# A fused attention and FP4 layer on one core: another order of the same steps on all five queues

## What is computed

```
xn = layernorm(x)
s  = attention block(xn): per head, scores = causal_kern[i-j] + qm[i] + km[j] + 0.15/sqrt(8) * qc[i].kc[j]
     (causal), softmax, times v; out projection; ln1(xn + .); ffn 256 -> 1024 -> 256 with gelu; ln2
     causal_kern comes from the mean of xn over each batch, a top-8 choice of 16 kernels, and a window
f  = fp4_linear(silu(fp4_linear(xn, w_gate)) * fp4_linear(xn, w_up), w_down)      256 -> 704 -> 256
     fp4_linear rounds both operands to FP4 (E2M1) in blocks of 16, with a scale per block
out = x + s * silu(f)
```

## Time and profile before

| | us |
|---|---|
| median of 3 runs | 1921.82 (1917.81 to 1922.19) |
| profiled execution, first to last instruction | 1916.1 |
| median above that span | 5.7 |
| first `out` matmul (L733) of all | 234.2 |
| one period of the mid part | 109.8 |
| from the last period to the end | 144.0 |

### The profile page before, as it was taken

How to read it: one execution, slowest core, us unless ns; L and a number is a source line. 1 busy time by engine, 2 the same in 40 slices (tenths; PEclk the granted TensorE clock), 3 DMA queues, 4 the chain that set the end, 5 groups by cost and what they waited for, 6 DMA issues and landing times.

```text
span 1916.1 us, 37547 instructions
## 1 busy us (share of the span) xinstructions
PE 1822.3 (95%) x12803; PEld 1311.7 (68%) x12803; DVE 1590.4 (83%) x5143; ACT 930.2 (49%) x1939; POOL 1095.4 (57%) x797
## 2 busy tenths in 40 slices
PE   7888999999999999999999999999999999999987
PEld 3335677777767767676776767677776767677766
DVE  6788899788888989888888978888897988888863
ACT  3635454544546354544635454453645445463542
POOL 2446657465556647464665746565664756466562
PEclk8999999999999999999999999999999999999999
DMA  5534233232322233232223323233222333322211
GB/s 156 165 96 114 64 91 83 75 110 75 99 75 79 76 82 115 75 90 73 91 74 93 93 75 110 64 102 79 83 77 75 110 84 91 75 85 74 61 57 34
DMA packets 138646, 166.69 MB, mean 87 GB/s; under 512 B 19757, under 2 KB 100654, under 8 KB 138452
## 3 DMA queue, kind: packets, MB, share of 16 engines
q1 hardware_dynamic: 138458, 164.30, 30.5%
HBM read 127.85 MB, written 36.41 MB: 86 GB/s over the span
## 4 chain that ended last, share of the span: by engine, by line
PE 50%; DVE 26%; issue 12%; POOL 4%; DMA 3%; ACT 3%; SPq 2%; DVEq 0%; POOLq 0%; ACTq 0%
PE ps L760 8%; PE ps L769 7%; PE ps L701 7%; PE ps L718 4%; DVE Pr L1067 3%; PE ps L624 3%; PE ps L597 3%; PE ps L733 3%; PE ps L658 3%; PE ps L674 2%; DVE nmax L1037 2%; POOL slot L1215 2%; PE ps L654 2%; DMA Tz<-kernel_rows 2%; DVE st L958 2%
## 5 line engine op out<-in xcount | busy, mean ns | idle before, releaser
L1176 POOL TENSOR_TENSOR Pr<-Pr,Tz 128x768 f32<-128x768 f32 (+2 forms) x384 | 477.6, 1273 | 233.8 <-ACT Pr L833 230.0
L1037 DVE CUSTOM_DVE_ANT_0 ps<-ps,future 128x512 f32<-128x512 f32 (+3 forms) x1024 | 474.5, 516 | 52.9 <-issue 51.8
L833 ACT ACTIVATE Pr<-ps 128x384 f32<-128x384 f32 x512 | 243.1, 489 | 345.2 <-PE ps L658 343.9
L760 PE MATMUL ps<-catT,w 128*128 128x256 f32 x1024 | 237.8, 380 | 0.7 <-ACT catT L896 0.7
L769 PE MATMUL ps<-w,gT 128*128 128x256 f32 x1024 | 232.9, 381 | 0.9 <-ACT gT L913 0.9
L624 PE MATMUL ps<-KS,QS 108*128 108x512 bf16 (+3 forms) x1024 | 215.0, 300 | 17.9 <-DVE nmax L1037 13.2
L822 ACT ACTIVATE ps<-ps 128x512 f32<-128x512 f32 x256 | 150.5, 588 | 137.7 <-PE ps L654 136.1
L1067 DVE SCALAR_TENSOR_TENSOR Pr<-ps,Tz 128x512 f32<-128x512 f32 x256 | 175.3, 685 | 46.2 <-ACT ps L822 41.0
L769 PEld LDWEIGHTS ps<-w,gT 128*128 128x128 f32 x1024 | 190.8, 190 | 25.7 <-ACT gT L913 1.3
L760 PEld LDWEIGHTS ps<-catT,w 128*128 128x128 f32 x1024 | 189.6, 190 | 26.2 <-ACT catT L896 0.9
L718 PE MATMUL ps<-wdT,hqT 128*128 128x256 f32 x768 | 179.5, 383 | 0.7 <-ACT hqT L872 0.7
(11 more groups left out here) (239 smaller groups left out, 3270.0 us busy)
## 6 DMA issues: line engine op xcount, KB each, us to landing
Tz<-kernel_rows SPq DMA_DIRECT2D x256, 256.0 KB, 3.6
KS<-k_parts SPq DMA_DIRECT2D x32, 384.0 KB
QS<-q_parts SPq DMA_DIRECT2D x64, 192.0 KB
hY<-in_x SPq DMA_DIRECT2D x19, 512.0 KB, 5.1
xn<-in_x SPq DMA_DIRECT2D x17, 512.0 KB, 3.8
out<-y SPq DMA_DIRECT2D x15, 512.0 KB, 2.9
q_parts<-q_sp SPq DMA_DIRECT2D x16, 384.0 KB, 3.0
k_parts<-k_sp SPq DMA_DIRECT2D x16, 384.0 KB, 2.4
```

The source lines that it names most:

```text
L760: ins = mm(dst[:, i * n:(i + 1) * n], w1[:, c, f * P:(f + 1) * P], catT[:, c, hf * n:(hf + 1) * n], start=c == 0, stop=c == KD - 1)
L833: inc(af(Pr[:, p % 4, e, at:at + wd], src[:, 0:wd], ACT.Exp), "a_exp")
L1037: ins = v.tensor_tensor_reduce(o, o, future[:, S - n:S], -1.0, 3e38, ALU.add, ALU.min, nmax[:, 2 * pl + e, it:it + 1])
L1176: ins = g.tensor_tensor(a, a, Tz[:, p % 2, :, P * j:P * j + PAST[j]], ALU.mult)
```

## The change

All five orders are written anew, in head, mid and end, with the same steps: none is added or removed, and no instruction within a step changes. `psum_plan` now counts the uses of each ring through the whole unrolled program, so a bank goes with the pair (batch, use) and no longer with (part, use); with 49 uses of the first ring, its two banks change places from one period to the next. `bank_for` and the `bank` functions look the bank up by batch.

The mid part whole:

```diff
     mid=dict(
         sync="""
-            T.0 load.1 T.1 T.2 xload T.3 mio.1 T.4 splitio T.5 load.0 T.6 T.7 fin mio.0
+            T.1 T.0 load.1 T.2 xload T.3 T.4 mio.1 T.5 splitio load.0 T.6 T.7 fin mio.0
         """,
         gpsimd="""
-            ln1 mul.0 lnb1 xnb mul.1 hq.0 mul.2 hr.0 projm.0 mul.3 hq.1 projm.1 hr.1 projm.2 xq xr mul.4 hq.2 mul.5
-            ln2 hr.2 fin mul.6 hq.3 mul.7 hr.3
+            ln1 lnb1 mul.0 xnb mul.1 hq.0 mul.2 hr.0 hq.1 mul.3 projm.0 projm.1 hr.1 projm.2 xq xr mul.4 hq.2 mul.5 hr.2
+            ln2 fin mul.6 hq.3 mul.7 hr.3
         """,
         vector="""
-            out.0 out.1 ln1 muld.0.0 silu.0.0 lnc1 silu.0.1 muld.0.1 mx.1.0.0 lnb1 mx.1.0.1 mx.1.0.2 muld.1.0 mx.1.0.3
+            out.0 out.1 ln1 muld.0.0 lnc1 silu.0.0 lnb1 muld.0.1 silu.0.1 mx.1.0.0 mx.1.0.1 muld.1.0 mx.1.0.2 mx.1.0.3
             silu.1.0 mx.1.0.4 mx.1.1.0 muld.1.1 mx.1.1.1 mx.1.1.2 mx.1.1.3 mx.1.1.4 muld.2.0 mx.1.2.0 mx.1.2.1 hq.0
-            mx.1.2.2 mx.1.2.3 norm mx.1.2.4 mx.1.3.0 muld.2.1 mx.1.3.1 mx.1.3.2 mx.1.3.3 mx.1.3.4 muld.3.0 mfin.1 hr.0
-            silu.1.1 f2.0 muld.3.1 proj.0 hq.1 f2.1 ctxt.0 proj.1 proj.2 muld.4.0 hr.1 xq muld.4.1 xr xr2 silu.2.0
-            muld.5.0 silu.2.1 hq.2 v.0 v.1 muld.5.1 f2.2 hr.2 mx.0.0.0 mx.0.0.1 f2.3 ln2 mx.0.0.2 mx.0.0.3 muld.6.0
-            silu.3.0 ctxt.1 muld.6.1 lnc2 lnb2 mx.0.0.4 mx.0.1.0 dn.0 silu.3.1 muld.7.0 mx.0.1.1 mx.0.1.2 mx.0.1.3
-            mx.0.1.4 hq.3 muld.7.1 mx.0.2.0 mx.0.2.1 mx.0.2.2 mx.0.2.3 mx.0.2.4 dn.1 ctxt.2 hr.3 mx.0.3.0 mx.0.3.1
-            dn.2 mx.0.3.2 mx.0.3.3 mx.0.3.4 mfin.0 ctxt.3 dn.3
+            mx.1.2.2 mx.1.2.3 norm mx.1.2.4 mx.1.3.0 muld.2.1 mx.1.3.1 mx.1.3.2 mx.1.3.3 mx.1.3.4 silu.1.1 muld.3.0
+            mfin.1 hr.0 muld.3.1 f2.0 hq.1 ctxt.0 proj.0 xq proj.1 proj.2 f2.1 hr.1 muld.4.0 silu.2.0 muld.4.1 xr xr2
+            silu.2.1 muld.5.0 v.0 hq.2 v.1 f2.2 muld.5.1 hr.2 f2.3 mx.0.0.0 mx.0.0.1 ln2 mx.0.0.2 muld.6.0 mx.0.0.3
+            silu.3.0 lnc2 mx.0.0.4 lnb2 muld.6.1 mx.0.1.0 dn.0 silu.3.1 mx.0.1.1 muld.7.0 mx.0.1.2 ctxt.1 mx.0.1.3
+            mx.0.1.4 hq.3 muld.7.1 mx.0.2.0 mx.0.2.1 mx.0.2.2 mx.0.2.3 mx.0.2.4 ctxt.2 dn.1 hr.3 mx.0.3.0 mx.0.3.1 dn.2
+            mx.0.3.2 mx.0.3.3 mx.0.3.4 mfin.0 ctxt.3 dn.3
         """,
         tensor="""
-            cT out.0 out.1 sc.0.0 gu.0.0 sc.0.1 gu.0.1 sc.0.2 sc.0.3 mx.1.0.0 mx.1.0.1 sc.0.4 gu.1.0 sc.0.5 mx.1.0.2
-            sc.1.0 hT sc.1.1 mx.1.0.3 sc.1.2 sc.1.3 mx.1.0.4 mx.1.1.0 sc.1.4 f1.0.0 mx.1.1.1 mx.1.1.2 f1.0.1 sc.1.5
-            sc.2.0 mx.1.1.3 mx.1.1.4 f1.0.2 mx.1.2.0 mx.1.2.1 f1.0.3 mx.1.2.2 mx.1.2.3 sc.2.1 sc.2.2 pv.0 sc.2.3
-            mx.1.2.4 mx.1.3.0 gu.1.1 mx.1.3.1 sc.2.4 xT.0 sc.2.5 sc.3.0 mx.1.3.2 xT.1 sc.3.1 ctxt.0 mx.1.3.3 mx.1.3.4
-            f2.0 mT.1 sc.3.2 sc.3.3 proj.0 sc.3.4 proj.1 proj.2 sc.3.5 f2.1 sc.4.0 sc.4.1 f1.1.0 tr.0.0 f1.1.1 f1.1.2
-            f1.1.3 sc.4.2 sc.4.3 gu.2.0 gu.2.1 sc.4.4 sc.4.5 v.0 sc.5.0 sc.5.1 v.1 f2.2 tr.0.1 sc.5.2 sc.5.3 f2.3
-            sc.5.4 sc.5.5 mx.0.0.0 mx.0.0.1 pv.1 sc.6.0 mx.0.0.2 mx.0.0.3 gu.3.0 sc.6.1 ctxt.1 sc.6.2 sc.6.3 mx.0.0.4
-            mx.0.1.0 sc.6.4 dn.0 sc.6.5 sc.7.0 gu.3.1 mx.0.1.1 pv.2 mx.0.1.2 sc.7.1 tr.1.0 mx.0.1.3 tr.1.1 mx.0.1.4
-            tr.2.0 sc.7.2 sc.7.3 mx.0.2.0 dn.1 sc.7.4 mx.0.2.1 sc.7.5 tr.2.1 mx.0.2.2 ctxt.2 mx.0.2.3 mx.0.2.4 dn.2
-            mx.0.3.0 mx.0.3.1 pv.3 mx.0.3.2 mx.0.3.3 xqT mx.0.3.4 tr.3.0 tr.3.1 ctxt.3 mT.0 dn.3
+            cT out.0 out.1 sc.0.0 gu.0.0 sc.0.1 gu.0.1 sc.0.2 sc.0.3 sc.0.4 gu.1.0 mx.1.0.0 mx.1.0.1 sc.0.5 sc.1.0 hT
+            sc.1.1 mx.1.0.2 mx.1.0.3 sc.1.2 sc.1.3 mx.1.0.4 mx.1.1.0 sc.1.4 f1.0.0 mx.1.1.1 mx.1.1.2 f1.0.1 mx.1.1.3
+            sc.1.5 sc.2.0 mx.1.1.4 f1.0.2 sc.2.1 mx.1.2.0 mx.1.2.1 sc.2.2 f1.0.3 sc.2.3 mx.1.2.2 mx.1.2.3 pv.0 mx.1.2.4
+            mx.1.3.0 gu.1.1 mx.1.3.1 xT.0 ctxt.0 sc.2.4 sc.2.5 mx.1.3.2 xT.1 sc.3.0 sc.3.1 mx.1.3.3 mx.1.3.4 f2.0 sc.3.2
+            sc.3.3 mT.1 proj.0 sc.3.4 proj.1 sc.3.5 f2.1 sc.4.0 proj.2 f1.1.0 f1.1.1 f1.1.2 sc.4.1 f1.1.3 gu.2.0 sc.4.2
+            tr.0.0 sc.4.3 gu.2.1 sc.4.4 sc.4.5 v.0 sc.5.0 f2.2 tr.0.1 sc.5.1 sc.5.2 v.1 sc.5.3 sc.5.4 f2.3 sc.5.5
+            mx.0.0.0 sc.6.0 mx.0.0.1 pv.1 mx.0.0.2 mx.0.0.3 gu.3.0 mx.0.0.4 tr.1.0 sc.6.1 sc.6.2 dn.0 sc.6.3 mx.0.1.0
+            sc.6.4 gu.3.1 mx.0.1.1 sc.6.5 sc.7.0 ctxt.1 mx.0.1.2 pv.2 mx.0.1.3 tr.1.1 sc.7.1 mx.0.1.4 tr.2.0 sc.7.2
+            sc.7.3 mx.0.2.0 dn.1 sc.7.4 mx.0.2.1 sc.7.5 ctxt.2 tr.2.1 mx.0.2.2 mx.0.2.3 mx.0.2.4 dn.2 mx.0.3.0 mx.0.3.1
+            pv.3 mx.0.3.2 mx.0.3.3 xqT mx.0.3.4 tr.3.0 tr.3.1 ctxt.3 mT.0 dn.3
         """,
         scalar="""
-            cT sc.0.0 vcopy silu.0.0 sc.0.1 silu.0.1 sc.0.2 sc.0.3 sc.0.4 sc.0.5 sc.1.0 hT silu.1.0 sc.1.1 sc.1.2
-            sc.1.3 sc.1.4 sc.1.5 sc.2.0 f1.0.0 f1.0.1 f1.0.2 f1.0.3 sc.2.1 sc.2.2 sc.2.3 ctxe.0 sc.2.4 xT.0 sc.2.5
-            silu.1.1 xT.1 sc.3.0 sc.3.1 mT.1 sc.3.2 sc.3.3 proj.0 projm.0 sc.3.4 proj.1 sc.3.5 proj.2 sc.4.0 sc.4.1
-            projm.1 projm.2 tr.0.0 f1.1.0 f1.1.1 f1.1.2 f1.1.3 sc.4.2 sc.4.3 sc.4.4 sc.4.5 silu.2.0 gscopy sc.5.0
-            sc.5.1 silu.2.1 sc.5.2 sc.5.3 sc.5.4 sc.5.5 tr.0.1 sc.6.0 ctxe.1 silu.3.0 sc.6.1 sc.6.2 sc.6.3 sc.6.4
-            sc.6.5 sc.7.0 dn.0 silu.3.1 ctxe.2 sc.7.1 tr.1.0 tr.1.1 sc.7.2 sc.7.3 sc.7.4 sc.7.5 tr.2.0 dn.1 tr.2.1
-            dn.2 ctxe.3 xqT tr.3.0 tr.3.1 mT.0 dn.3
+            cT vcopy sc.0.0 sc.0.1 silu.0.0 sc.0.2 sc.0.3 sc.0.4 silu.0.1 silu.1.0 sc.0.5 sc.1.0 sc.1.1 hT sc.1.2 sc.1.3
+            sc.1.4 sc.1.5 sc.2.0 sc.2.1 f1.0.0 f1.0.1 f1.0.2 f1.0.3 sc.2.2 ctxe.0 sc.2.3 xT.0 sc.2.4 sc.2.5 xT.1 gscopy
+            silu.1.1 sc.3.0 sc.3.1 sc.3.2 sc.3.3 mT.1 sc.3.4 sc.3.5 proj.0 proj.1 proj.2 sc.4.0 projm.0 projm.1 f1.1.0
+            f1.1.1 projm.2 f1.1.2 f1.1.3 sc.4.1 silu.2.0 sc.4.2 sc.4.3 sc.4.4 silu.2.1 sc.4.5 tr.0.0 sc.5.0 sc.5.1
+            sc.5.2 sc.5.3 sc.5.4 sc.5.5 tr.0.1 sc.6.0 ctxe.1 silu.3.0 sc.6.1 sc.6.2 sc.6.3 sc.6.4 dn.0 tr.1.0 silu.3.1
+            sc.6.5 sc.7.0 ctxe.2 sc.7.1 tr.1.1 sc.7.2 sc.7.3 sc.7.4 sc.7.5 tr.2.0 dn.1 tr.2.1 dn.2 ctxe.3 xqT tr.3.0
+            tr.3.1 mT.0 dn.3
         """,
```

Of the head, VectorE's stretch in which `pro:xr`, `pre:wr.2` and `pre:ws.2` stand:

```diff
-            first:mx.1.0.4 pre:fr.14 pre:fr.15 pre:kw pre:ws.2 pro:xr first:norm pro:xr2 pre:wr.2 first:mx.1.1.0
-            first:mx.1.1.1 first:mx.1.1.2 first:mx.1.1.3 pre:soft first:mx.1.1.4 first:xq first:proj.0 first:proj.1
...
+            pre:fr.15 first:mx.1.0.4 pre:kw first:mx.1.1.0 pre:ws.2 first:mx.1.1.1 first:mx.1.1.2 pre:wr.2 pro:xr
+            first:norm pro:xr2 first:mx.1.1.3 pre:soft first:mx.1.1.4 first:xq first:proj.0 first:proj.1 first:mx.1.2.0
```

The plan of the banks:

```diff
 PARTS = dict(head=dict(pre=-2, pro=-1, first=0), mid=dict(mid=0), end=dict(last=B - 1, tail=B))
+TURNS = [("head", 0)] + [("mid", b) for b in range(1, B - 1)] + [("end", B - 1)]
...
-    uses = {p: [(w, u) for w, s in orders[p] for u in kinds(s)] for p in PARTS}
-    place, before = {}, {}
-    tail = {p: dict(zip(banks, uses[p][-len(banks):])) for p in PARTS}
-    for b in banks:
-        assert tail["head"].get(b, (0, 0))[1] == tail["mid"][b][1], "banks differ between iterations"
-    for p in PARTS:
-        last = {}
-        if p == "mid":
-            last = {b: (u, -1) for b, (w, u) in tail["mid"].items()}
-        for i, (w, u) in enumerate(uses[p]):
-            bank = banks[(i - len(uses[p])) % len(banks)]
-            place[w, u] = bank
-            at = PARTS[p][w]
-            if p == "end" and bank not in last:
-                before[w, u] = (tail["mid"][bank][1], B - 2 - at)
-            elif bank in last:
-                before[w, u] = (last[bank][0], last[bank][1] - (at if p != "mid" else 0))
-            last[bank] = (u, at)
+    uses = [(at, u) for p, at in TURNS for w, s in orders[p] for u in kinds(s) for at in [at if p == "mid" else PARTS[p][w]]]
+    ahead = sum(len(kinds(s)) for w, s in orders["head"])
+    place, before, last = {}, {}, {}
+    for i, (at, u) in enumerate(uses):
+        bank = banks[(i - ahead) % len(banks)]
+        place[at, u] = bank
+        if bank in last:
+            before[at, u] = last[bank]
+        last[bank] = (u, at)
     return place, before
 
...
-        def bank_for(ring, released, eng, u, which, b):
+        def bank_for(ring, released, eng, u, b):
 
             place, before = plans[ring]
-            if (which, u) in before:
-                earlier, ago = before[which, u]
-                released(eng, earlier, b + ago)
-            return ps[:, place[which, u], :]
+            if (b, u) in before:
+                released(eng, *before[b, u])
+            return ps[:, place[b, u], :]
 
```

More of the change, by code:

```diff
@@ L81 @@
+            pre:ld.basis pre:px.4 pre:ld.c0 pre:px.6 pre:rz pre:ld.c1 pre:px.7 pro:splitio pre:px.8 pre:ones pre:px.9
+            pre:px.10 pro:load.0 pre:px.11 pre:px.12 pre:px.13 pre:px.14 pre:px.15 pro:load.1 pre:ld.c2 pre:ld.w_rest
+            first:xload pro:mio.0 pre:rows first:T.0 first:T.1 first:splitio first:T.2 first:T.3 first:mio.1 first:T.4
```

(20 more changed lines are left out.)

210 lines of the change are left out of this document (98 added, 112 removed).

## The result

The change makes the kernel faster by a little: median 1913.64 us (1911.02 to 1920.29, 16 runs) against 1922.01 (1916.75 to 1925.96, 16 runs) before, ratio 0.9962 with an interval from 0.9950 to 0.9973. By the ratio that is 7.3 us less; the two medians are 8.4 apart. Forecast were 1906.3 and 0.8%.

What follows compares the result with a forecast made beforehand. TensorE was taken to lose 6.3 us a period in four places, partly to VectorE. Gains of 0.35 + 0.25 + 0.7 - 0.4 = 0.9, 13.5 over 15, plus 1.5 head and 0.5 end, gave 1906.3 (own range 1898 to 1913, wide 1889 to 1921).

Steps and rivals of the forecast that it cites:

- The first stretch: From `out` to `f1.0.0`: ScalarE's exponential of `sc.1.1` ahead of the copies of `hT` removes a wait, gaining 0.35 a period.
- `hT`'s 0.6: Moving VectorE's `lnb1` ahead lets `hT` gain 0.6, but none reaches `f1`, since `mx.1.1.0` waits for VectorE's `mx.1.0.3`.
- `xT.1`: `ctxt.0` and both `xT` now stand between scores and their exponentials: 0.25 of a 0.33 loss gained a period.
- thin places: Tight spots in the new order, such as `sc.0.4`, `mT.1` and `proj.2`: 0.4 a period subtracted, between 0 and 0.9.
- The middle: `T.5` and `silu.2.0` moved ahead: VectorE enters its dense stretch 0.9 earlier, of which TensorE gets 0.7 a period.
- `hq.2`: VectorE step in the dense stretch that lost 0.63; walked to lose 0.6 to 1.3, no gain counted, 0.7 for the range.
- more: Rival: thin places cost nothing, TensorE regains nearly all its waits for VectorE, 1.9 a period, 1891 us; chance 0.18.
- The ring of banks: PSUM banks: both rings have two and four banks before and after, so no effect; 0.6 a period if cover were gone.
- slower: Rival: `gu.2.1`'s second half waits for the bank `silu.2.0` frees, margin 0.3; 1940 us, or 1929 held likelier; chance 0.12.
- `lnc1` blocked: Rival: `lnc1` on VectorE is blocked beside GpSimd's rstd, losing 0.55 a period, so 1914.5 us; chance 0.10.
- Head 1.5, end 0.5: Outside the periods: gains of 1.5 us in the head, 0.6 at `pro:xr` and 0.9 from other moves, and 0.5 at the end.
- 5.7 around the span: Time added outside the profiled span, as before: 1900.6 plus 5.7 gives 1906.3, the profiled execution standing for the median.

Runs made afterwards that it cites:

- sc11_back: Changed kernel with ScalarE's exponential of `sc.1.1` behind the copies of `hT` again: usual period 109.35 us, against 109.37 in the changed kernel.
- front_old: Changed kernel with the old order in the front two thirds of the mid part and in SP's queue: period 109.41 us; timed again 1913.61 us, ratio 0.9961.
- tail_old: Changed kernel with the old order in the last third of the mid part, new order ahead of it: period 109.79 us.
- j_late: Changed kernel with one unread VectorE pass added behind the scales of `hq.3` in each mid period: period 109.78 us, 0.41 more.
- t0_first: Changed kernel with SP's `T.0` ahead of `T.1` again in the mid part: 14 periods in 1530.92 us; timed again 1913.87 us, ratio 0.9965.
- plan_only: Old kernel, all orders as before, with only the new plan of the banks: 1922.25 us, ratio 0.9993 to before.
- s2_back: Changed kernel with `silu.2.0` put back behind `muld.4.1`, `xr` and `xr2` on VectorE: 2006.01 us, period 115.83.
- nolock: Changed kernel with the two short passes of the scales written as scalar_tensor_tensor with a constant column as second operand: period 109.35 us.
- end_only: Old kernel with the new plan of the banks and the new end alone: 1919.72 us, ratio 0.9988 to before.

## Why the prediction was wrong

The direction was right, the size was not: 0.38% for 0.8%. 1913.6 lies just outside the forecast's own range of 1898 to 1913, inside the wide one, and on the side that held 0.74. Step by step:

- **The first stretch, 0.35.** Wrong. The wait for ScalarE went, but `f1.0.0` came only 0.14 earlier, and sc11_back, with the same 18.54, shows that the exponential has no part in it: `mx.1.1.0` waits for VectorE in any case. The prediction used this very limit to strike out `hT`'s 0.6, and did not hold ScalarE's edit against it.
- **`xT.1`, 0.25, and the thin places, 0.4.** They lie in the front, and the whole new front is worth 0.03 to 0.06 a period by front_old and tail_old. How much each of them was is not shown.
- **The middle, 0.7. This is the step that failed.** "VectorE enters its dense stretch 0.9 earlier" came true, even as 1.47. But the 0.7 that was to reach TensorE did not: at `silu.3.0` 0.04 of the lead was left. "VectorE is dense from 957.95 on" was read from one period, one in which VectorE was late by its wait of 0.62. A VectorE that comes earlier meets GpSimd at `hq.2`, whose blocked passes end with GpSimd's and took 0.47 more than before, and then TensorE and ScalarE, with waits of 0.19 at `v.1` and 0.08 at the tanh of `gu.3.0`. In the six periods of before in which `T.5` was in time, the same stretch has waits of about 0.17 and 0.33, and those periods are no shorter. So of the 0.9, the 0.62 of `T.5` was worth nothing already there. The lead would have had to reach the last third; j_late shows that 0.61 of VectorE's time counts 0.41 there.
- **`hq.2`.** The walk was right: it lost 1.1 (0.56 + 0.54), within 0.6 to 1.3. But before it had lost 0.63, and the sum put the difference, 0.47, at nothing (the range held 0.7 for it).
- **The last third.** The prediction gave it no gain of its own; all that it has on it is "VectorE's work is the same", in the rival "more". It made 0.40 of the 0.45. The block at `hq.3` (0.59 in the period shown of before) was not looked at, nor was the gap that `ctxt.1` fills.
- **SP's queue.** `T.1` ahead of `T.0` was in the diff and was not costed. In the profiled execution it costs 1.8 us in all, as t0_first shows.
- **The ring of banks at nothing.** Right by plan_only. The rival "slower" had the right mechanism and the right point, and a margin of 0.69 for the 0.3 walked. Its price was too low: s2_back lost 6.5 a period for 4.69 of stall, the rest by the clock.
- **`lnc1` blocked.** It did not happen: L960 began at 900.74 while the rstd pass ran from 900.27 on, and its four took 1.66 in all, as before (1.67). The section on the hardware shows such passes blocked beside a larger pass of GpSimd.
- **Head 1.5, end 0.5.** The head gave nothing that shows (ratio 1.0007), the end 1.9 by the traces.
- **5.7 around the span.** Wrong. The changed kernel's execution took 1912.32 for a span of 1910.5, so 1.8 lies around it. The execution profiled before was one of the short ones. It took about 1916.1 + 1.8 = 1917.9, which is 3.9 under the median; I put this difference down to what lies around the span. The forecast change of the span, 15.5, does not hang on it; 6.6 of it came.

Put together from the table: 14 periods 4.7 less than in the three other kernels with the old mid part (1532.73 against 1537.43), 0.2 in the last period, 1.7 in the rest: 6.6. The measured 7.3 has an interval from 5.2 to 9.6.

What stays open is how the 0.40 divides between the small pieces behind `silu.3.0` and the block at `hq.3`.

## What to carry to other kernels

Two engines that hand work to each other all the time have several places where they meet. A lead of one is worth only what it still is at the next place, and that at the last one. So walk a lead to the end of the period before it is priced, and ask at each step what the other engine has ready. If a wait comes in some periods and not in others, compare their lengths first: the trace of before showed by this that `T.5` was worth nothing. Cutting the period in two, with the old order in front or behind, told in two runs what single edits had not. And an edit in one engine's order, moved alone, can cost far more than it measures (6.5 and 2.9 us a period here), since the other engines' orders were written to fit it.

## What the runs showed of the hardware

**Blocks of VectorE by GpSimd.** The short passes stay blocked when their second operand comes from SBUF (0.77 where 0.23 is needed). The Trainium skill, "SBUF — State Buffer", section "Who interferes with whom", says that a VectorE instruction with two SBUF inputs contends with a GpSimd instruction that reads SBUF. With that nolock agrees. L960, with two such inputs, was not held up beside GpSimd's pass over four elements a partition (four in 1.66). Beside passes over 768 elements it was, in the last period of the changed kernel:

```profile
1852.37 3.22 DVE L960 SCALAR_TENSOR_TENSOR y<-y,mv,row_ln_g 128x256 f32<-128x256 f32 x4
...
1853.45 3.97 POOL L1164 TENSOR_TENSOR Pr<-Pr,Tz 128x768 f32<-128x768 f32 x3 [2.22 <-ACT Pr L821]
```

The four took 3.22 for 1.66. So it matters which pass of GpSimd stands beside it. That it is the amount the pass reads is not shown, nor is any limit between 4 and 768 elements.

**The length of the head.** In the twenty profiled executions the first `cT` starts between 232.5 and 242.8, with the old head (232.45 to 240.52, four) as with the new one. Most of the difference arises early. Twelve matmuls with the old head, first in end_only (`cT` at 233.43), then in plan_only (240.52):

```profile
18.38 7.23 PE L1543 MATMUL ps<-ctxT,Tz 6*128 6x512 f32 x12
```

```profile
18.33 10.60 PE L1545 MATMUL ps<-ctxT,Tz 6*128 6x512 f32 x12
```

They took 0.60 and 0.88 each in the mean. By their starts most of them follow the one before at one of two distances, 0.43 or 0.85, which stand as the two levels of TensorE's clock do, 2.4 and 1.2 GHz. In plan_only all twelve are at the slow one, in end_only eight at the fast one and then four at the slow one. For those four the granted clock says so: it reads 0.50 from 22 to 26. For the twelve of plan_only it doesn't: it reads 1.00 from 18 to 30. So the record of the granted clock can read full while matmuls go at half the rate. In plan_only TensorE works without a pause from 14.81 until past 32, and its matmuls are slow for the first 17 us of that; in end_only the first fast one starts at 18.38. The next six matmuls of this shape start at 42.77 and at 48.03 in the two, so 5.3 of the 7.1 us between the heads are there by then. What decides when the fast level comes was not tried.
